# W_out's columns one slot sooner, the residual's load one entry later, and other lists of work between VectorE, ScalarE and GpSimd

## The reference

```python
proj = xn @ W_in.T; u, gate = split(proj)          # xn = layernorm(x)
u = silu(causal depthwise conv(u) + conv_b)
dt, Bm, Cm = split(u @ Wx.T); each rmsnorm'ed
delta = softplus(dt @ Wdt.T + dt_bias)
state = exp(delta * A) * state + (delta * u) * B_t   # for every token, D x N states
y_t = sum_n state * C_t
y = (y + u * D_param) * silu(gate)
s = y @ W_out.T
g = silu(ffn(xn))                                  # silu(x Wg) * (x Wu), then W_down; inner size 1376
x = x + s * g
```

## Time and profile before

| | us |
|---|---|
| median of three runs | 1111.97 |
| the profiled execution | 1112.61 |
| its span | 1110.8 |
| PE busy | 1024.4 (92%) |
| DVE busy | 1035.5 (93%) |
| POOL busy | 967.4 (87%) |
| ACT busy | 719.0 (65%) |
| L1191 DVE, the 512 scans | 597.1, 1.209 each |
| L913 POOL, dBu | 603.8, 2.391 each |
| L866 POOL, add_part | 181.1, 1.293 each |
| L1107 DVE, add_state | 238.6, 0.735 each |

### The profile page before, as it was taken

The page is one execution under the profiler, slowest core; times in us unless marked ns, Lnnn a source line. Parts: engine busy times, 40 slices in busy tenths (PEclk is TensorE's granted clock), DMA queues, the critical chain, the costliest instruction groups (busy, mean ns, idle before and its releaser), DMA issues.

```text
span 1110.8 us, 14875 instructions
## 1 busy us (share of the span) xinstructions
PE 1024.4 (92%) x5040; PEld 753.5 (68%) x5040; DVE 1035.5 (93%) x1237; ACT 719.0 (65%) x1177; POOL 967.4 (87%) x531
## 2 busy tenths in 40 slices
PE   6969988899989999999999999998998999999877
PEld 5848766666758886675857887576766888555444
DVE  4679999899899999999999999999999999999995
ACT  4666766777576877477676786477576685456540
POOL 3648998999989999779979999968998999979981
PEclk9879999799989999999999999999999999999989
DMA  4626754443324654343233564334332543335511
GB/s 148 224 97 217 258 196 172 153 161 109 104 88 151 224 181 151 115 161 124 97 120 111 184 217 157 133 123 142 125 109 93 183 163 138 114 114 170 167 42 57
DMA packets 46619, 160.93 MB, mean 145 GB/s; under 512 B 5358, under 2 KB 5614, under 8 KB 37072
## 3 DMA queue, kind: packets, MB, share of 16 engines
q1 hardware_dynamic: 46400, 159.93, 42.2%
q10 hardware_dynamic: 144, 0.07, 0.0%
HBM read 135.59 MB, written 24.38 MB: 144 GB/s over the span
## 4 chain that ended last, share of the span: by engine, by line
PE 31%; POOL 28%; DVE 22%; issue 15%; ACT 3%; DMA 1%; SPq 0%; DVEq 0%; POOLq 0%
POOL sb_dBu L913 17%; DVE sb_h L1191 12%; PE pj L1252 10%; PE pj L1464 7%; PE hT L1554 6%; POOL sb_yT L866 6%; DVE sb_yT L1107 5%; DVE sb_un L989 2%; POOL sb_v L848 2%; PE pj L1572 2%; POOL sb_u L852 1%; PE pj L1498 1%; PE pj L1257 1%; PE pj L1529 1%; POOL sb_w_sp L831 1%
## 5 line engine op out<-in xcount | busy, mean ns | idle before, releaser
L913 POOL TENSOR_TENSOR sb_dBu<-sb_v,sb_bb 128x1024 f32<-128x1024 f32 x254 | 603.8, 2391 | 41.3 <-DVE sb_h L1191 28.5
L1191 DVE TENSOR_TENSOR_SCAN sb_h<-dA,sb_dBu 128x512 f32<-128x512 f32 x512 | 597.1, 1209 | 18.7 <-POOL sb_dBu L913 15.5
L673 ACT ACTIVATE dA<-sb_delta,sb_apar 128x512 f32<-128x512 f32 x510 | 344.9, 689 | 221.8 <-DVE sb_h L1191 219.9
L1252 PE MATMUL pj<-sb_x_hi,sb_w_sp 128*128 128x512 f32 x1208 | 344.6, 409 | 21.7 <-DVE sb_un L989 12.2
L1554 PEld LDWEIGHTS hT<-sb_ident,sb_h 128*128 128x128 f32 x2048 | 240.2, 144 | 127.3 <-issue 45.6
L1554 PE MATMUL hT<-sb_ident,sb_h 128*128 128x128 f32 x2048 | 283.5, 280 | 43.8 <-DVE sb_yT L1107 35.1
L1252 PEld LDWEIGHTS pj<-sb_x_hi,sb_w_sp 128*128 128x128 f32 x1208 | 223.2, 193 | 69.7 <-DVE sb_un L989 8.7
L1107 DVE SCALAR_TENSOR_TENSOR sb_yT<-hT,sb_cs,sb_yT 128x512 f32<-128x512 f32 x336 | 238.6, 735 | 10.0 <-PE hT L1554 9.4
L866 POOL TENSOR_TENSOR sb_yT<-sb_yT,sb_part 128x512 f32<-128x512 f32 x140 | 181.1, 1293 | 25.3 <-ACT sb_part L779 25.3
L1252 PE MATMUL pj<-sb_x_lo,sb_w_sp 128*128 128x512 f32 x604 | 167.3, 400 | 0.0
L779 ACT ACTIVATE sb_part<-hT,sb_cs_act 128x512 f32<-128x512 f32 x140 | 95.6, 683 | 95.4 <-PE hT L1554 85.3
(11 more groups left out here) (148 smaller groups left out, 774.4 us busy)
## 6 DMA issues: line engine op xcount, KB each, us to landing
sb_w_sp<-w_cache SPq DMA_DIRECT2D x55, 1024.0 KB, 4.8
sb_ring<-w_ring SPq DMA_DIRECT2D x67, 512.0 KB, 3.6
sb_bb<-b_rows SPq DMA_DIRECT2D x128, 256.0 KB, 3.4
w_cache<-sb_w_sp SPq DMA_DIRECT2D x19, 1024.0 KB, 4.9
sb_xio<-x SPq DMA_DIRECT2D x7, 1024.0 KB, 7.6
out<-sb_xio SPq DMA_DIRECT2D x3, 1024.0 KB, 5.6
sb_xio<-x SPq DMA_DIRECT2D x4, 256.0 KB, 3.3
out<-sb_xio SPq DMA_DIRECT2D x4, 256.0 KB, 2.0
```

Of the source, the lines that this page charges most:

```text
L673: nc.scalar.activation(dA[g % 2][:, :], delta[:, j, :], ACT.Exp, scale=apar[:, j, n:n + 1]).then_inc(dA_done, 1)
L913: nc.gpsimd.tensor_tensor(dBu[:, dbu_buffer(s), :, :], v[:, j:j + 2, :], bb[:, i % B_RING, :].unsqueeze(1).to_broadcast([P, 2, T]), ALU.mu ...
L1191: nc.vector.tensor_tensor_scan(h[:, i % 2, 2 * part + e, :], dA[g % 2][:, :], dBu[:, dbu_buffer(s), e, :], 0.0, ALU.mult, ALU.add).then_in ...
L1252: done = nc.tensor.matmul(bank[:, :], w[:, kk * P:(kk + 1) * P], xs[:, kk, :], start=(p == 0), stop=(p == len(products) - 1))
```

## The change

Four things are changed. S_OUT becomes 22, which moves W_out's columns (slots 22 to 29), what VectorE does with their results (slots 26, 28, 30, 32), and the loads that wait for them. The residual's load goes behind the load after OUT0 + 1; with S_OUT = 22, OUT0 is used before the last x transposes are done. `handed_over` gives units 21 and 22, c = 2, back to VectorE in the first sequence, and takes c = 1 of units 17 and 18 from it in the three others. GpSimd's step_size and inputs of the second half of the channels stand in slots 17, 23, 25 and 27 of the first sequence, and inputs(b + 1, 0) in slot 62 of every sequence but the last.

```diff
-S_OUT = 23
+S_OUT = 22
...
     if first:
-        return () if u < FIRST_UNIT else (0, 2) if 11 <= u < 23 else (0,)
+        return () if u < FIRST_UNIT else (0, 2) if u < 21 else (0,)
+    if u in (17, 18):
+        return 0, 1, 2
...
     if not first:
-        after["used", OUT0] = "xres"
+        after["used", OUT0 + 1] = "xres"
...
-                    if s == 14:
+
+                    if s == (17 if first else 14):
                         step_size(b, 2)
-                    if s == 16:
+                    if s == (23 if first else 16):
                         inputs(b, 2)
-                    if s == 18:
+                    if s == (25 if first else 18):
                         step_size(b, 3)
-                    if s == 20:
+                    if s == (27 if first else 20):
                         inputs(b, 3)
...
-                    if s == SLOTS - 3:
+                    if s == SLOTS - 2:
                         inputs(b + 1, 0)
```

## The result

| | before | after |
|---|---|---|
| median, us (12 runs each) | 1112.58 | 1115.99 |
| the profiled execution | 1112.61 | 1115.76 |
| its span | 1110.8 | 1114.0 |

A forecast was written before the change was run, and what follows sets the result against it. No one engine bounds it: three are busy at once, and which is late in which slot counts. +8.0 + 3.4 - 0.8 - 1.75 - 2.9 - 0.8 = +5.15: 1112.61 becomes 1117.8, median 1117.1; range 1107 to 1121.

The forecast's parts named there:

- The forecast case: Whole kernel: slower, 1117.1 us on the median, mainly by W_out's moved column and the transposes queued behind it; chance 0.45.
- W_out, +8.0: Slots 22 to 36: moved column waits for its bank, delaying transposes; +2.25 in sequences 1 and 2, +3.5 in the last.
- step by step walk through the queues: TensorE and VectorE followed slot by slot: VectorE waits 2.4 us in slot 25, 1.2 in 27; slot 36 2.25 later.
- pace of 4.31 us a slot: TensorE's pace after slot 25: column 3.44 plus two transpose groups 0.87, against a VectorE slot of 3.5 to 4.2.
- The clock, +3.4: TensorE's pauses of 2.45 to 2.85 us before W_out's column lower its clock in two of three sequences, 1.7 us each.
- GpSimd's slots, -0.8: First sequence: waits in slots 17, 19, 21 go (3.4 us); products of slots 26 to 28 come late; net -0.8.
- Sums given back, -1.75: First sequence: VectorE pays 0.65 in slots 45 and 47; stalls of 1.84 and 1.20 us in slots 50, 51 vanish.
- Slot 62, -0.8: Product for the next sequence one slot later: stalls in slots 62 and 1 go; 0 into sequence 1, -0.4 each later.
- Sums given away, -2.9: Units 17 and 18, slots 36 and 38: VectorE saves 1.3 us in sequences 1 and 2, 0.3 in the last.
- rival C: Slots 37 to 39: ScalarE's two partial-result buffers jam on the third sum, delaying decays and scans; 1124 us, chance 0.08.
- The residual's load, 0: Load goes out about one TensorE slot later; data are wanted in slot 34, eight slots on, so it costs nothing.
- B: VectorE recovers the pause of slot 25 up to TensorE's extra 0.87 a sequence: 1108.3 us, to 1104.7; chance 0.14.

The follow-up runs named there:

- e3: The changed kernel with the half column of slot 22 issued in slot 23, behind that slot's transposes: 1110.98 us, ratio 0.9991.
- e2: The kernel before with only W_out's columns moved to slots 22 to 29 and the residual's load one entry later: 1123.98 us, ratio 1.0112.
- e6: e1 with GpSimd's step sizes and inputs of the first sequence back in slots 14, 16, 18 and 20: 1107.22 us, ratio 0.9964.
- e10: e1 with the residual's load one entry later, as in the change: 1101.63 us, ratio 0.9899.
- e7: e1 with units 21 and 22 of the first sequence giving GpSimd two sums again, as before: 1107.04 us, ratio 0.9947.
- e5: e1 with the product for the next sequence back in slot 61: 1107.70 us, ratio 0.9959.
- e4: e1 with units 17 and 18 giving away two sums as before, not three: 1105.26 us, ratio 0.9940.
- e12: The kernel of e9 unchanged, run once more: 1102.17 us, ratio 0.9906.
- e9: e1 with GpSimd's last step size and inputs (first sequence) in slots 28, 29; units 17, 18 give three sums only in sequences 1, 2: 1101.89 us, ratio 0.9914.
- e1: The changed kernel with W_out's columns back in slots 23 to 30 and the residual's load back one entry: 1106.23 us, ratio 0.9958.

## Why the prediction was right, and where its sum was not

The forecast case came in: slower by 3.15 us in the profiled executions where the sum said 5.15, and for the reason named first.

- **W_out, +8.0.** Measured 2.2 in each of sequences 1 and 2 when the clock stays (2.22 in sequence 2; 3.79 less 1.6 for the clock in sequence 1), and 3.5 in the last to slot 34: 7.9 in all. The step by step walk through the queues held: the column behind the gate operation, the wait of 2.4 us in slot 25 (2.38 in sequence 2, 2.44 in the last), 1.2 in slot 27 (1.22). e3 shows that the queue order makes this wait. Two sizes were off. In the last sequence 0.4 us more are lost behind slot 34, where the walk ended, after the pause in slot 33, so 8.3. And the pace of 4.31 us a slot is 4.39 by the two starts that are named for it (436.22 - 430.96 - 0.87).
- **The clock, +3.4.** Half of it. One of the three pauses before the column was followed by a fall (1.6 us), that of 2.49 us in sequence 1; the same pause in sequence 2 and that of 2.90 us in the last were not. In e2 two of three. The step that failed is the one that ordered the pauses by length: "2.85 is at the row and 2.45 nearer to it than to 1.5". In the two kernels with this order, three of four pauses of 2.48 to 2.52 us were followed by the lower clock, and neither of the two of 2.90. Nor was the one row of 2.86 us a rule: that pause, in slot 61, comes back in all 14 traces, three times each (2.86 to 2.92 us), and the clock fell before its end or within 1.6 us of it in 35 of 42. "For a pause of 2.45 no row decides" overlooked one in the trace before, of 2.32 us in slot 53 of the last sequence, with the clock at 0.50 from 0.9 us after its end on:

```profile
1051.35 2.52 PE L1554 MATMUL hT<-sb_ident,sb_h 128*128 128x128 f32 x12 [2.32 <-DVE sb_yT L1107]
...
1052.20:1055.20 3.00, 1.67 (x8) 0.92 (x6) 3.00 (x4) 1.65 (x3) 3.00 (x2) 0.50 0.31 85
```

The Trainium skill (TensorE: Matmul & The Clock Gate, Part 1, on oscillation), by which none of these pauses should have lowered it, is contradicted by three columns that took 5.2 to 5.4 us and not 3.67.
- **GpSimd's slots, -0.8.** Measured 0 (e6: 0.2 worse; e10 is 1.0 better than e6, since its lower clock ended sooner). The stalls of slots 26 and 27 came as counted (1.24 and 0.41 for 1.4 and 0.6), the third in 28 did not; but the wait for the transpose in slot 27 (1.53 us) was not seen, since only VectorE's feed was counted on. The late split weight feeds TensorE's column too, and that column came after a pause of 3.44 us at the lower clock.
- **Sums given back, -1.75.** -2.5 (e7: 2.4). The two stalls went as said; 0.6 more was won in slots 54 and 55, where a wait of 0.62 us for dA went with them.
- **Slot 62, -0.8.** -0.9, -1.1 and -1.5, so -3.5 (e5: 2.9 by undoing it). The step that failed is "TensorE ... sets VectorE's slot 10 anyway: 0 there", and for the others the trust in the idle records of the earlier trace rows, 0.21 + 0.28 us. The distance from transposes to transposes tells more. Before, hT starts at 597.16, 601.16 and 605.50: 4.00 and 4.34 us a slot. After:

```profile
595.69 1.03 PE L1557 MATMUL hT<-sb_ident,sb_h 128*128 128x128 f32 x8
...
599.31 1.03 PE L1557 MATMUL hT<-sb_ident,sb_h 128*128 128x128 f32 x8
...
602.94 1.03 PE L1557 MATMUL hT<-sb_ident,sb_h 128*128 128x128 f32 x8
```

That is 3.62 and 3.63 us. So 0.37 + 0.71 = 1.1 us were lost there, more than twice the idle time that the records name: the restarts after a pause are slower too (hT 1.22 for 1.03).
- **Sums given away, -2.9.** -1.3, -1.3 and -0.5 came (e4), but in the last sequence +1.3 for slot 51 was missing from the account. ScalarE's two buffers did not jam (rival C). The prediction asked whether GpSimd has room in the slot of the sums, 2.77 us, and not whether it finds some again before the next thing that needs it.
- **The residual's load, 0.** The stretches say 0; the medians leave it open (e10).
- **The rivals' sums.** Two are wrong as added. B with all of the 3.4 us is 1105.7, not 1104.7, since 0.8 of them is in 1108.3 already; C is 1117.1 + 2.9 + 6 = 1126, not 1124. The range and the forecast don't rest on them.
- Not in the sum: 1.9 us in the last slots (3.57-3.63), where a column ran at the lower clock (5.03 us from 1079.27) and slot 62 waited 0.96 us. Slot-23 kernels have from -0.2 (e10) to 2.1 (e6) of it, so W_out's place doesn't make it.

The sum came out near in part by luck, because its errors offset each other: the clock (1.8), slot 62 (2.7) and the sums given back (0.8) turned out better than forecast, GpSimd's slots (0.9), slot 51 (1.3) and the last slots (1.9) worse.

## What to carry to other kernels

A block moved forward in an in-order queue takes its wait with it, and the block that it passes pays: before moving, ask when its buffer comes free, and who needs what is then queued behind it. If the hole in front of it is made by the same consumer that frees its buffer, moving it fills nothing. A helper engine's slack has to be followed to its next appointment, not just to the slot where the work is added, and a lost rhythm is read from the distance between repeated instructions, not from the idle time beside them.

## What was not expected of the hardware

After pauses of TensorE of 2.48 to 2.52 us before the same instruction the granted clock fell to the lower level three times of four, and after 2.90 us not once of two; a fall there cost 1.6 to 1.7 us. Right ahead of the shorter pauses TensorE did transposes of h and of x, ahead of the longer ones only those of h. But the pause in slot 61 was followed by a fall three times of three in e12 and once of three in e9, which is the same code; and in slot 25 of the last sequence of e1 and e6 the clock fell without any pause over 1.3 us. What decides was not separated.

Runs of one kernel differ by up to 10.8 us (the kernel after: 1107.71 to 1118.47), and much of that stands before the fifth slot of the first sequence, in work that none of these kernels changes. e9 and e12 are the same code; in their profiled executions slot 0 starts at 61.65 and 63.87 us, slot 4 at 80.5 and 84.0, and the granted clock from 40 to 60 us is 1.00 and 0.79; the clock by slices (tenths, 40 slices) differs at the left. First e9, then e12:

```profile
PEclk9989999899999999999999999999999999999989
```

```profile
PEclk9869999799999999999999999999999999999989
```

So differences of 1 to 3 us between kernels were read from stretches of the trace, and the medians alone could not have told e1, e4, e5, e6 and e7 apart.
